# The second attention's softmax denominators: a matmul against ones in place of columns, copies and transposes

## The reference

```
x = layernorm(x + attention1(x))     # 16 heads of 16, every head weighs its own row's v
x = layernorm(x + attention2(x))     # per batch: a router picks 4 of 16 heads of 64
# attention2, for each picked head, over the whole 2048 rows:
score = softmax(Q K^T / 8);  O = score V;  out = O @ Wo + bo
```

## Time and profile before

| | |
|---|---|
| time, median of 3 runs (lowest to highest) | 3679.16 us (3677.96 to 3679.68) |
| time of the profiled execution | 3678.28 us |
| span of the profiled execution | 3676.2 us |
| mean granted TensorE clock | 0.983 of full |

### The profile page before, as it was taken

How to read it: one execution, slowest core, us unless ns; L and a number is a source line. 1 busy time by engine, 2 the same in 40 slices (tenths; PEclk the granted TensorE clock), 3 DMA queues, 4 the chain that set the end, 5 groups by cost and what they waited for, 6 DMA issues and landing times. The chain is left out here.

```text
span 3676.2 us, 45342 instructions
## 1 busy us (share of the span) xinstructions
PE 3442.9 (94%) x14524; PEld 1301.0 (35%) x14524; DVE 3328.6 (91%) x5273; ACT 2863.5 (78%) x3137; POOL 1872.8 (51%) x1299
## 2 busy tenths in 40 slices
PE   8999998899999999899999999899999999899998
PEld 3444443332232234343332324343332324343333
DVE  7999999999999998889999998879999998567776
ACT  5999999878888887778888887778888887333333
POOL 4344343414454547455454547445454546658775
PEclk9999999899999999899999999999999999999999
DMA  5222221300000002101010001101000100100000
GB/s 168 92 86 90 86 86 61 87 21 18 18 29 15 23 18 63 54 18 29 18 29 14 26 18 58 59 18 29 18 26 13 29 18 26 43 1 12 12 12 12
DMA packets 117214, 142.83 MB, mean 39 GB/s; under 512 B 33394, under 2 KB 100466, under 8 KB 116978
## 3 DMA queue, kind: packets, MB, share of 16 engines
q1 hardware_dynamic: 116978, 139.95, 12.4%
HBM read 89.55 MB, written 50.33 MB: 38 GB/s over the span
## 5 line engine op out<-in xcount | busy, mean ns | idle before, releaser
L1163 ACT ACTIVATE scores<-scores,nmax 128x2048 f32<-128x2048 f32 x1024 | 2042.4, 1996 | 297.4 <-DVE scores L1391 286.1
L1018 PE MATMUL ps<-stack 96*128 96x512 bf16 x4852 | 1314.0, 388 | 116.2 <-DVE scores L1391 86.2
L1391 DVE TENSOR_SCALAR_CACHE_REDUCE scores<-ps,lows 128x1024 f32<-128x1024 f32 x1024 | 1274.8, 1277 | 45.1 <-PE ps L1018 42.5
L920 POOL TENSOR_TENSOR facc<-facc,probs 128x1024 f32<-128x1024 f32 x443 | 1048.0, 2366 | 487.0 <-ACT probs L1302 416.6
L1391 DVE TENSOR_SCALAR_CACHE_REDUCE scores<-ps 128x1024 f32<-128x1024 f32 x1024 | 1214.6, 1217 | 52.2 <-PE ps L1018 46.9
L1018 PEld LDWEIGHTS ps<-stack 96*128 96x128 bf16 x4852 | 374.5, 99 | 1174.6 <-DVE scores L1391 687.8
L1448 DVE TENSOR_REDUCE smax<-ps 128x2 f32<-128x1024 f32 x512 | 620.3, 1219 | 131.4 <-PE ps L1083 129.9
L1083 PE MATMUL ps<-fk,fq 64*128 64x512 f32 x2048 | 562.5, 631 | 48.5 <-DVE smax L1448 30.9
L1098 PE MATMUL ps<-fq,fk 64*128 64x512 f32 x2048 | 550.2, 615 | 10.0 <-DVE smax L1448 4.1
L1118 PE MATMUL ps<-probs,vals 128*64 128x512 f32 x2048 | 527.4, 612 | 0.2
L1302 ACT ACTIVATE probs<-ps 128x1024 f32<-128x1024 f32 x384 | 383.2, 1012 | 66.9 <-PE ps L1101 66.4
(11 more groups left out here) (136 smaller groups left out, 2335.5 us busy)
## 6 DMA issues: line engine op xcount, KB each, us to landing
stack<-qk_levels SPq DMA_DIRECT2D x768, 64.0 KB, 2.2
qk_levels<-fk SPq DMA_DIRECT2D x64, 384.0 KB, 2.4
probs<-in_L_attn_x SPq DMA_DIRECT2D x16, 512.0 KB, 3.9
v_rows<-vals SPq DMA_DIRECT2D x16, 512.0 KB, 2.6
vrows<-v_rows SPq DMA_DIRECT2D x16, 512.0 KB, 3.4
res<-in_L_attn_x SPq DMA_DIRECT2D x16, 512.0 KB, 3.9
x_rows<-y SPq DMA_DIRECT2D x16, 512.0 KB, 2.9
res<-x_rows SPq DMA_DIRECT2D x16, 512.0 KB, 3.9
```

The source lines that it names most:

```text
L920: pool.tensor_tensor(total, total, probs[:, slot, :], ALU.add).then_inc(facc_ready, 1)
L1018: last = pe.matmul(bank(banks[i]), stack[0:SK, hd % 2, 0, t * P:(t + 1) * P], stack[0:SK, hd % 2, 1, col:col + CH], start=True, stop=True)
L1163: act.activation(row, row, ACT.Exp, bias=nmax[:, k % LOWS:k % LOWS + 1], scale=-1.0, accum_out=esum[:, b % 2, t, hd:hd + 1]).then_inc(exp_ ...
L1391: dve.tensor_scalar(scores[:, k % ROW_SLOTS, half * TILE:(half + 1) * TILE].rearrange("p (a n) -> p a n", a=2), two_banks(banks), 1.0, fir ...
```

## The change

D becomes two (in the last group four) fp32 matmuls with a 128x64 block of ones as weights and 512 columns of `facc` moving, one for each head of the pair, into 64 rows each: the sums come out already spread along the head's rows. There is no transpose and no R on PE. In all groups but the last ACT copies the bank to `fsum`, takes the logarithm and the exponential of its negative, which gives an approximate reciprocal in `foT`, and POOL makes one Newton step (three instructions) and multiplies by `oacc`. This holds for the last batch too, where DVE did the multiplication. In the last group DVE takes the reciprocal of the whole 128x512 bank and multiplies. The planner's units, costs and lists follow, so that the order of all engines is planned anew.

```diff
-PARTS = {..., "FO": 4, "D": 2}
+PARTS = {..., "FO": 4}
...
-                main += [(spot, ("D",) + was)] * (step == 3) + [(spot, ("R",) + was)] * (step == 6)
+                main += [(spot, ("D",) + was)] * (step == 3)
...
-            fill(("D", b, g), 1.85 * len(sums), 1, sums, dve("D", b, g))
-            unit(dve("D", b, g), 0.2, [pe("D", b, g)] + ([pool("D", *one)] if one else []))
-            unit(pool("D", b, g), 0.6, [dve("D", b, g)] + ([pe("R", *one)] if one else []))
-            fill(("R", b, g), 0.75, 1, [pool("D", b, g)], (act if b + 1 < B else dve)("R", b, g))
+            end = b * GROUPS + g + 1 == B * GROUPS
+            fill(("D", b, g), 0.89 * len(sums), 1, sums, dve("D", b, g) if end else act("D", b, g))
             free = [pe("OP", b + 1, NCH - 1)] if b + 1 < B and c + 1 == NCH else []
             last = pool("V", b, g, BURSTS - 1) if b + 1 < B else act("V", b, g, 0)
-            if b + 1 < B:
-                unit(act("R", b, g), 0.5, [pe("R", b, g), pe("V", b, g, STEPS - 1)] + free)
-                unit(pool("R", b, g), 1.25, [act("R", b, g), last])
+            if end:
+                unit(dve("D", b, g), 4.2, [pe("D", b, g), pe("V", b, g, STEPS - 1)])
+                unit(dve("R", b, g), 0.68, [dve("D", b, g), last, pool("R", *one)])
             else:
-                unit(dve("R", b, g), 0.68, [pe("R", b, g), last] + ([pool("R", *one)] if g == 0 else []))
+                unit(act("D", b, g), 1.7, [pe("D", b, g), pe("V", b, g, STEPS - 1)] + free + ([pool("R", *one)] if one else []))
+                unit(pool("R", b, g), 5.2, [act("D", b, g), last])
...
-    mode = {"S": 1, "T": 1, "BC": 1, "V": 2}
+    mode = {"S": 1, "T": 1, "BC": 1, "V": 2, "D": 2}
...
@@ GpSimd
-                    pool.tensor_tensor(foT(c)[:, pair, :], foT(c)[:, pair, :], oacc[:, g % 2, :], ALU.mult
-                    pool.tensor_copy(frec_wide[:, :, :, :], frec[:, :, :].unsqueeze(3).to_broadcast([P, TPC, 2, FD])
+                    pool.wait_ge(fsum_rec, k + 1)
+                    pool.tensor_tensor(fsum[:, :], fsum[:, :], rec, ALU.mult).then_inc(recip_step, 1)
+                    pool.tensor_scalar(fsum[:, :], fsum[:, :], -1.0, 2.0, ALU.mult, ALU.add).then_inc(recip_step, 1)
+                    pool.tensor_tensor(rec, rec, fsum[:, :], ALU.mult).then_inc(recip_step, 1)
+                    pool.tensor_tensor(rec, rec, oacc[:, g % 2, :], ALU.mult).then_inc(foT_ready, 1)
@@ TensorE
-                        for t in pieces(kind, piece, TPC):
-                            for h in range(2):
-                                for i in shares:
-                                    last = pe.matmul(ps[:, banks[0], 2 * t + h:2 * t + h + 1],
-                                                     facc[:, i, h * CH + t * P:h * CH + (t + 1) * P], ones[:, :],
-                        for t in range(TPC):
-                            last = pe.transpose(ps[:, banks[0], t * P:(t + 1) * P],
-                                                frec_wide[:, t, :, :].rearrange("p h n -> p (h n)"), ident[:, :])
+                        for i in shares:
+                            for h, rows in two:
+                                last = pe.matmul(ps[rows, banks[0], :], ones[:, :], facc[:, i, h * CH:(h + 1) * CH],
+                                                 start=(i == shares[0]), stop=(i == shares[-1]))
@@ ScalarE
-                    act.activation(foT(c)[:, pair, :], bank(banks[0]), ACT.Copy).then_inc(r_copied, 1)
+                    act.wait_ge(foT_ready, k)
+                    act.activation(fsum[:, :], bank(banks[0]), ACT.Copy).then_inc(fsum_ready, 1)
+                    act.wait_ge(fk_ready, (b + 1) * PAIRS * NCH)
+                    act.wait_ge(fv_ready, (b + 1) * NCH)
+                    act.activation(rec, fsum[:, :], ACT.Ln).then_inc(fsum_log, 1)
+                    act.activation(rec, rec, ACT.Exp, scale=-1.0).then_inc(fsum_rec, 1)
@@ VectorE (the last group alone)
+                    dve.reciprocal(rec, bank(banks[0])).then_inc(last_rec, 1)
+                    dve.tensor_tensor(rec, rec, oacc[:, g % 2, :], ALU.mult).then_inc(foT_ready, 1)
```

More of the change, by code:

```diff
@@ L67 @@
 HALVES = ("VP", "FV", "OP", "FO")
-PARTS = {"QP": 2, "KP": 2, "FK": 2, "FQ": 2, "VP": 4, "FV": 4, "OP": 4, "FO": 4, "D": 2}
+PARTS = {"QP": 2, "KP": 2, "FK": 2, "FQ": 2, "VP": 4, "FV": 4, "OP": 4, "FO": 4}
 GAP = 0.6
 URGENT = ("M", "J", "AT", "OT", "OP", "OPh", "X1", "RT")
-PATIENT = {k: 20 for k in ("QP", "KP", "VP", "XT", "FK", "FQ", "FV", "OP", "FO", "OT", "X1", "D", "R", "RT")}
+PATIENT = {k: 20 for k in ("QP", "KP", "VP", "XT", "FK", "FQ", "FV", "OP", "FO", "OT", "X1", "D", "RT")}
 PATIENT.update({"FK": 30, "FQ": 30})
@@ L308, in plan @@
                 if b + 1 == B:
-                    unit(dve("C", *t), 1.2, after + [act("BC", b, g)])
-                    after = [dve("C", *t)]
+                    unit(dve("C", *t), 1.2, after + [act("BC", b, g)] + ([dve("C", b, g, n - 1)] if n else []))
+                    after = [dve("C", *t)] + ([act("T", b, g, n - 1)] if n else [])
                 unit(act("T", *t), 1.0, after)
@@ L614, in build @@
         ROUTE_STEPS = 11
+        RECIP_STEPS = 3
         QK_DMAS, V_DMAS = 4 * FH // PAIRS, 2 * FH
@@ L675, in build @@
                    ("ACT", "VPh"): v_half, ("ACT", "VP"): v_copied, ("ACT", "QP"): q32_ready, ("ACT", "FQ"): fq_ready, ("ACT", "FVh"): vals_half, ("ACT", "FV"): vals_copied,
-                   ("DVE", "S"): smax_ready, ("DVE", "D"): frec_ready, ("DVE", "R"): foT_ready, ("ACT", "R"): r_copied}
+                   ("DVE", "S"): smax_ready, ("DVE", "D"): last_rec, ("ACT", "D"): fsum_ready}
         block = ctx.enter_context(nc.Block())
@@ L1008, in _ @@
                     else:
-                        pe.wait_ge(read_by[was[:2]], group_no(*was[2:]) + 1 if was[:2] == ("DVE", "R") else nth[was])
+                        pe.wait_ge(read_by[was[:2]], nth[was])
                 if kind == "A":
@@ L1121, in _ @@
                         last.then_inc(pv_done, 1)
-                    elif kind == "D":
+                    else:
                         if (b, g) == last_group:
@@ L1266, in _ @@
                     act.activation(rstd[:, i % 2, :], rstd[:, i % 2, :], ACT.Exp, scale=-0.5).then_inc(rstd_ready, 1)
-                elif kind == "R":
+                elif kind == "D":
                     b, g = at
-                    pair, c = g % PAIRS, g // PAIRS
+                    k, pair, c = group_no(b, g), g % PAIRS, g // PAIRS
+                    rec = foT(c)[:, pair, :]
+                    act.wait_ge(foT_ready, k)
+                    act.activation(fsum[:, :], bank(banks[0]), ACT.Copy).then_inc(fsum_ready, 1)
                     act.wait_ge(fk_ready, (b + 1) * PAIRS * NCH)
                     act.wait_ge(fv_ready, (b + 1) * NCH)
-                    if c + 1 == NCH:
+                    if c + 1 == NCH and b + 1 < B:
                         act.wait_ge(filled, fill_no["OP", b + 1, NCH - 1])
-                    act.activation(foT(c)[:, pair, :], bank(banks[0]), ACT.Copy).then_inc(r_copied, 1)
+                    act.wait_ge(fsum_ready, k + 1)
+                    act.activation(rec, fsum[:, :], ACT.Ln).then_inc(fsum_log, 1)
+                    act.wait_ge(fsum_log, k + 1)
+                    act.activation(rec, rec, ACT.Exp, scale=-1.0).then_inc(fsum_rec, 1)
                 elif kind == "M":
@@ L1481, in _ @@
                     b, g = at
[L1482 to L1484 removed]
+                    rec = foT(g // PAIRS)[:, g % PAIRS, :]
+                    dve.wait_ge(fk_ready, (b + 1) * PAIRS * NCH)
+                    dve.wait_ge(fv_ready, (b + 1) * NCH)
+                    dve.reciprocal(rec, bank(banks[0])).then_inc(last_rec, 1)
                 else:
                     b, g = at
[L1487 removed]
+                    rec = foT(g // PAIRS)[:, g % PAIRS, :]
+                    dve.wait_ge(last_rec, 1)
                     dve.wait_ge(part_ready, nth["ACT", "V", b, g, 0])
                     dve.wait_ge(foT_ready, group_no(b, g))
[L1490 to L1492 removed]
+                    dve.tensor_tensor(rec, rec, oacc[:, g % 2, :], ALU.mult).then_inc(foT_ready, 1)
 _INS = ["x", "w_in", "b_in", "w_out", "b_out"]
```

45 lines of the change are left out of this document (15 added, 30 removed).

## The result

The changed kernel takes 3706.44 us (median of 4 runs, 3703.25 to 3707.70), the kernel before 3678.86 on the same chip (4 runs): a ratio of 1.0074, interval [1.0062, 1.0086]. It is 27.6 us slower; 3664 was predicted, with 3684 as the upper end. The profiled execution took 3703.25, its span 3701.5.

A forecast was written before the change was run, and what follows sets the result against it. DVE was taken to bound the middles, PE the last batch and the stretches after the first two seams: 3678.28 - 9.2 - 3.1 - 0.9 - 3 + 1.0 - 0.3 = 3662.8, plus 0.9 for the median, rounded 3664 us; range 3646 to 3684.

The forecast's parts named there:

- a gain of 3: Middles of the first three batches: DVE sheds the 128x8 reciprocal, saving 3 us (bounds 2 and 25).
- PE's time comes back in the middle too: Rival, middles: the new order recovers half or all of DVE's 21.8 us idle, 3653 or 3642; chance 0.12.
- POOL's block in the last batch: Last batch: seven blocks ask 41 of POOL's 134 us idle time; costed at nothing.
- The slower rival: Last batch: POOL's 5.9 us more per group delays adds, then slots, then C and V; 3705, chance 0.13.
- The end's +1.0: End: the second-last group's 6.5 us block pushes POOL's adds 2.1 late, 1.1 covered; +1.0 us (0 to 2.1).
- After the seams, -3.1 us: After the first two seams: PE sets the pace, one group each saves 1.53, 3.1 us in all (0 to 3.1).
- a seam that takes longer because the block sits ahead of POOL's norms: Seams: listed among the signs that would show the forecast wrong; no size given.
- in place of 0.9: Third seam: only D is on the chain, 1.88 - 0.94, saving 0.9 us.
- Last batch, -9.2 us: Last batch: PE sets the pace; 6 x 1.53 us per group saves 9.2 us (bounds 3.0 and 10.7).
- ACT, costed at nothing: First three batches: one ACT copy becomes three instructions, net +1.2 us per group, covered by three row slots.
- The bound of 19 us: Middles: cost of ACT's added work if the row slots gave no cover, 1.2 x 16 = 19 us.
- The end's own chain: Last group, from D's start to the multiplication's end: 7.5 us instead of 7.8, -0.3 (bounds -4.4 and +1.1).

The follow-up runs named there:

- e_gate3: Changed kernel with its planner keeping query projections (FQ) and output projections (FO) behind the fourth V of the group after: 3680.71 us, ratio 1.0002.
- v2_light: e_gate3 without the Newton step, the logarithm reading the PSUM bank directly (two ACT instructions, one POOL), planner costs adjusted: 3664.61 us, ratio 0.9954.
- e_poolnorm: e_gate3 with the last batch's three middle output layer norms (chunks 0 to 2) on POOL instead of DVE: 3666.07 us, ratio 0.9954.
- e_seam: e_gate3 with POOL's two bias additions in the seams held until DVE has done the first attention's last layer norm: 3674.86 us, ratio 0.9984.
- b_pool: Kernel before, with four more 128x256 multiplications on POOL in each group of the last batch: 3696.49 us, ratio 1.0041.
- e_nolog: Changed kernel with ACT's logarithm and exponential replaced by a one-column copy and its bank copy scaled, plan kept, denominators not inverted: 3697.65 us (one run).
- b_act: Kernel before, with a logarithm and an exponential put ahead of ACT's copy in each group of the first three batches: 3694.44 us (one run).

## Why the prediction was wrong

- **Costed at nothing: what R's place on PE held back.** The prediction counted the transposes' 0.59 us and R's bank, and noted that every order is planned anew. It didn't ask what stood behind R in the in-order list: FQ and FO. Without R both became free right behind D, and the plan placed them there, among the fills on which DVE lives in the middle; FO, which the prediction put six steps of V after D, starts 9 us after it. It cost some 17 us in the middles where a gain of 3 was forecast, and e_gate3 gave all of it back. The rival "PE's time comes back in the middle too" failed in this order, as DVE's idle time grew; with the gates and the lighter block it comes true in part, 16 us (v2_light).
- **Costed at nothing: POOL's block in the last batch.** The step asked whether POOL has room (it has) and who waits for POOL's results. It didn't ask whether another engine's instruction can be stopped by POOL merely running. The slower rival named the place, but not the mechanism: at these stops no slot of `probs` was short; DVE's layer norm was stopped. That its time, 3705, is nearly the measured one is chance, as 17 us of the loss lie in the middles. Its own mechanism shows at the third norm of e_poolnorm. The end's +1.0 for the second-last group's block missed the same thing: the third stop, 4.9 us, lies there. The Trainium skill (SBUF — State Buffer, "SBUF: two separate sides") says that VectorE and GpSimd share one pair of ports as an exclusive lock, held for a whole instruction, which a VectorE instruction needs in a two-port mode or with two inputs in SBUF. The rows agree for POOL's TENSOR_TENSOR: 2.28, 2.27, 2.19 us for instructions of 0.16, each ending with POOL's. They don't for one form of POOL's TENSOR_SCALAR (last section). DVE's reads of PSUM were not stopped: the score evictions (L1388, L1445) kept their 1.22 to 1.28 us.
- **The trace of before had it.** The normalisation on DVE by line and shape, once in the last batch and once in the third seam, where POOL adds beside it: 408 ns against 1676 for the same instruction. I read this line's mean over the whole run, 796, which mixes both.

```profile
L819 DVE TENSOR_SCALAR y<-y,mv,rstd 128x256 f32<-128x256 f32 x12 | 4.1, 408 | 0.1
```

```profile
L819 DVE TENSOR_SCALAR y<-y,mv,rstd 128x256 f32<-128x256 f32 x12 | 19.4, 1676 | 0.1
```

- **After the seams, -3.1 us.** It became a loss of 5.5. The wrong signal listed, "a seam that takes longer because the block sits ahead of POOL's norms", was near but not it: the new order put POOL's bias additions beside DVE's norm (e_seam gives back 3.8 and 3.5). With them held, e_seam gains 1.1 and 1.8 us on the kernel before over the two seams, 2.8 of the 3.1 forecast: the term was right, the stop hid it. At the third seam 2.9 came back in place of 0.9, but b_pool, unchanged there, moved by 2.8.
- **Last batch, -9.2 us: right in kind, hidden by the stops.** Between the norms the kernel gained from the start: +19.4 to +14.1 in three groups, 1.8 us a group against the 1.53 forecast. With the norms out of the way (e_poolnorm) D goes from -2.4 to -17.9 against before over seven groups; that is more than the 10.7 that the change alone was bounded by, as the kernel before kept its norms on DVE. The change's plan also makes each C and T of the last batch wait for the one before it, two lines that the diff shown above doesn't have; no run takes them away.
- **ACT, costed at nothing: wrong in the order as planned.** There the activations made a quarter of the middles' loss (e_nolog). With e_gate3's order the middles gained 3.1, 1.9 and 1.5 us, 6.5 in place of the 3 predicted, with all three activations; what v2_light gains beyond that, some 9, may be in part theirs. The bound of 19 us was real: b_act shows 16.4.
- **Prices.** New D 1.07 busy against 0.94; POOL's two-immediate instruction 0.62 against 2.4, so the block was 4.7 and not 6.5, the lower bound; last D 1.94 against 3.4, as the granted clock was 0.95 there and not 0.64; the reciprocal 3.36 against 3.3, by the slope of two rows. The estimate of 4.3 from the Trainium skill's repeat count (VectorE: DVE Perf Modes, "First, the fixed hardware budget") would have been 28% too high. The end's own chain gained 1.7 us in place of 0.3.

## What to carry to other kernels

Before an instruction is taken out of an in-order list, look at what stands behind it there: it may be the gate that keeps other work out of the way, and its removal is a change of order, not only of its own duration. Before work is put on GpSimd "where it is idle", look at which of VectorE's TENSOR_TENSOR and TENSOR_SCALAR instructions on SBUF operands alone run at that time; compare such an instruction's mean between stretches where GpSimd runs and where it doesn't, in the trace of before. When a large saving on the busiest engine turns up in its busy time and not in the span, go by one landmark per group through both timelines: the places of loss stand out in steps.

## What the runs showed of the hardware

How far POOL stops DVE depends on both instructions. On DVE's side the layer norm's TENSOR_TENSOR and TENSOR_SCALAR, with SBUF operands alone, were stopped; its BATCH_NORM_STATS2, which also reads and writes SBUF alone, kept 0.40 to 0.43 us in the changed kernel beside POOL's TENSOR_TENSOR (50 instructions) as without POOL. On POOL's side, TENSOR_TENSOR and TENSOR_SCALAR with two immediates stopped DVE to their end (above). POOL's TENSOR_SCALAR with two operands per partition, four in a row for 4.94 us in the first seam of the kernel before, hardly did: the DVE norm beside it took 1.69 in place of 1.38 for its four normalisations, and at most 0.34 in place of 0.17 for a small instruction. Why the two forms differ was not tried.

```profile
1496.56 4.94 POOL L819 TENSOR_SCALAR y<-y,mv,rstd 128x256 f32<-128x256 f32 x4
```

```profile
1498.08 1.69 DVE L819 TENSOR_SCALAR y<-y,mv,rstd 128x256 f32<-128x256 f32 x4
```
